# Moving twelve tiles of a mixture-of-experts matmul out of a recurrent loop and behind it

## What is computed

```python
def cell(h, x):
    gi = x @ W_ih + b_ih
    gh = h @ W_hh + b_hh
    i_r, i_z, i_n = jnp.split(gi, 3, axis=-1)
    h_r, h_z, h_n = jnp.split(gh, 3, axis=-1)
    r = jax.nn.sigmoid(i_r + h_r)
    z = jax.nn.sigmoid(i_z + h_z)
    n = jnp.tanh(i_n + r * h_n)
    h_new = (1.0 - z) * n + z * h
    return (h_new, h_new)
...
logits = xf @ router_w + router_b
S = jax.nn.softmax(logits, axis=-1)
G, idx = jax.lax.top_k(S.T, k)          # k = 256 tokens for each expert
out = jnp.einsum('ekh,hd->ekd', tokens, expert_w) + expert_b
y = zeros.at[idx].add(G[..., None] * out)
x = x + y
```

## Time and profile before

| | us |
|---|---|
| median of 3 executions | 1153.72 (1152.94 to 1154.68) |
| the profiled execution | 1152.81 |
| its span, first to last instruction | 1150.7 |
| TensorE matmul busy | 1135.9 (99% of the span) |
| VectorE busy | 770.9 (67%) |
| ScalarE busy | 363.2 (32%) |

### The profile page before, as it was taken

One profiled execution on the slowest core, in us unless ns is written; L12 is line 12 of the kernel. 1 busy time (PEld: TensorE's weight loads), 2 busy tenths in 40 slices (PEclk: granted clock), 3 DMA queues, 4 the chain that ended last, 5 costly groups with the idle time before them and its releaser, 6 DMA issues.

```text
span 1150.7 us, 63227 instructions
## 1 busy us (share of the span) xinstructions
PE 1135.9 (99%) x28287; PEld 1002.7 (87%) x28287; DVE 770.9 (67%) x4245; ACT 363.2 (32%) x1366; POOL 6.8 (1%) x31
## 2 busy tenths in 40 slices
PE   8999999999999999999999999999999999999998
PEld 5888888888999999999999999999999999999872
DVE  3677667676666666666666666666666666666886
ACT  1333333333333232323333333333333333332440
POOL 2000000000000000000000000000000000000000
PEclk9999999999999999999999999999999999999999
DMA  6311000111111001111110011111000000000208
GB/s 242 86 22 21 13 15 20 21 22 22 21 22 22 16 10 21 21 22 22 22 22 10 17 21 22 22 22 22 16 11 11 13 12 13 4 4 3 59 17 280
DMA packets 80261, 36.93 MB, mean 32 GB/s; under 512 B 69987, under 2 KB 69987, under 8 KB 79990
## 3 DMA queue, kind: packets, MB, share of 16 engines
q1 hardware_dynamic: 77648, 28.66, 10.4%
q10 hardware_dynamic: 2342, 4.24, 1.1%
HBM read 24.49 MB, written 8.39 MB: 29 GB/s over the span
## 4 chain that ended last, share of the span: by engine, by line
PE 95%; DVE 2%; DMA 1%; issue 0%; SPq 0%; ACT 0%; DVEq 0%
PE gates L429 58%; PE gates L414 29%; PE ffn_ps L472 5%; PE gates L472 3%; DMA whh<-in_L_cond_W_hh 1%; PE log_ps L481 1%; DVE wih L717 1%; PE log_ps L554 0%; SPq L234 0%; SPq L237 0%; DVE thr_upper L738 0%; DVE reached L733 0%; PE gates L574 0%; DVE wih L764 0%; DVE u L616 0%
## 5 line engine op out<-in xcount | busy, mean ns | idle before, releaser
L429 PE MATMUL gates<-whh,tok 128*16 128x192 f32 x16384 | 716.1, 326 | 2.8 <-DMA whh<-in_L_cond_W_hh 2.4
L429 PEld LDWEIGHTS gates<-whh,tok 128*16 128x16 f32 x16384 | 601.1, 124 | 57.7 <-DMA whh<-in_L_cond_W_hh 3.2
L414 PE MATMUL gates<-wih,xT 128*32 128x192 f32 x8192 | 384.3, 327 | 0.1
L414 PEld LDWEIGHTS gates<-wih,xT 128*32 128x32 f32 x8192 | 289.7, 111 | 42.7 <-issue 0.8
L616 DVE SCALAR_TENSOR_TENSOR u<-th,gates 128x64 f32<-128x64 f32 x512 | 113.3, 221 | 302.3 <-ACT th L326 302.3
L326 ACT ACTIVATE th<-gates 128x128 f32<-128x128 f32 x512 | 140.0, 273 | 443.2 <-PE gates L429 443.2
L331 ACT ACTIVATE n_t<-v 128x64 f32<-128x64 f32 x512 | 131.2, 256 | 277.7 <-DVE v L620 277.7
L632 DVE STREAM_TRANSPOSE nT<-n_t 128x64 f32<-128x64 f32 x512 | 123.8, 242 | 0.0
L623 DVE STREAM_TRANSPOSE zT<-th 128x64 f32<-128x64 f32 x512 | 121.6, 237 | 0.0
L620 DVE SCALAR_TENSOR_TENSOR v<-u,gates 128x64 f32<-128x64 f32 x512 | 113.2, 221 | 8.8
L641 DVE SCALAR_TENSOR_TENSOR tok<-new_n,z_h 128x32 f32<-128x32 f32 x512 | 110.7, 216 | 8.7
(11 more groups left out here) (111 smaller groups left out, 147.9 us busy)
## 6 DMA issues: line engine op xcount, KB each, us to landing
x_in<-in_x SPq DMA_DIRECT2D x248, 32.0 KB, 2.1
xs<-in_x SPq DMA_DIRECT2D x26, 256.0 KB, 3.6
out<-tok SPq DMA_DIRECT2D x16, 256.0 KB, 3.8
out<-tok ACTq DMA_DIRECT2D x16, 256.0 KB, 3.9
wih<-in_L_cond_W_ih SPq DMA_DIRECT2D x4, 768.0 KB, 7.1
whh<-in_L_cond_W_hh SPq DMA_DIRECT2D x4, 768.0 KB, 12.9
whh<-in_x SPq DMA_DIRECT2D x6, 256.0 KB, 4.7
we<-in_L_ffn_expert_w SPq DMA_DIRECT2D x1, 1024.0 KB, 5.4
```

What stands on the lines that cost most here:

```text
L414: nc.tensor.matmul(gates[q % 2][a][Q * j:Q * (j + 1), IN:HN].rearrange("b (g k c) -> b g k c", g=G, k=KH), xT[:, n % 2, kc, first:first + ...
L429: mm = nc.tensor.matmul(gates[t // S % 2][a][Q * j:Q * j + rows, R_:GC].rearrange("b (g k c) -> b g k c", g=G, k=KH), columns, by_tile(whh ...
```

## The change

Four things are edited. `IN_LOOP` becomes 0, so no unit stands in the loop but for the 6 in each of the last two steps; the presets and stores of ScalarE in the loop go, and the one preset that the last steps need is issued at step 252. With `IN_LOOP = 0` the first 9 tiles are the stored ones (`IN_PSUM = 9`), and 23 tiles are read from PSUM. `PSUM_PLACES` gives these 23 their places in the order of the sums: the first five, every second one up to place 20, and the last ten. PE's wait for the layer's weights moves from step 64 to step 32.

```diff
--- before.py
+++ after.py
@@ -43,9 +43,8 @@
     PAD = P
 
 
-    IN_LOOP = 12
+    IN_LOOP = 0
     UNITS = K * 4
-    FIRST = T - IN_LOOP * UNITS
     BANKS = 5
 
     LAST_UNITS, SOFTMAX_UNITS, ROUND_UNITS, SHORT_UNITS = 6, 28, 9, 4
@@ -53,7 +52,7 @@
     EVACUATED = 9
     IN_PSUM = IN_LOOP + EVACUATED
 
-    PSUM_PLACES = [0, 1, 2, 3, 4, 9, 14, 18, 22, 27, 31]
+    PSUM_PLACES = [i for i in range(NT) if i < 5 or i % 2 == 0 or i > 21]
     stored_tiles, psum_tiles = iter(range(IN_PSUM)), iter(range(IN_PSUM, NT))
     OUT_ORDER = [next(psum_tiles if i in PSUM_PLACES else stored_tiles) for i in range(NT)]
     FFN_LOADS = (4 + NI) * 16
@@ -356,18 +355,13 @@
                 if t % S == S - 1 and t // S + 2 < NB:
 
                     set_biases(t // S + 2)
-                if t == FIRST - 2:
+                if t == T - 4:
                     act.wait_ge(ffn_w_loaded, FFN_LOADS)
                     preset_ffn(0)
-                if t > FIRST and (t - FIRST) % UNITS == 0:
-                    store_ffn((t - FIRST) // UNITS - 1)
-                if t >= FIRST and (t - FIRST) % UNITS == 2 and (t - FIRST) // UNITS + 1 <= IN_LOOP:
-                    preset_ffn((t - FIRST) // UNITS + 1)
 
 
             for n in range(IN_LOOP + 1, IN_LOOP + BANKS - 1):
                 preset_ffn(n)
-            store_ffn(IN_LOOP - 1)
             preset_ffn(IN_LOOP + BANKS - 1)
             act.wait_ge(shifted, 1)
             nc.scalar.activation(scores, scores, ACT.Exp).then_inc(soft_exp, 1)
@@ -526,10 +520,9 @@
             for t in range(T):
                 tt, q, s = t % TT, t // S, t % S
                 step(t)
-                if t == FIRST:
-                    pe.wait_ge(ffn_w_loaded, FFN_LOADS)
                 if t and t % (QUAD * TT) == 0:
                     if t == QUAD * TT:
+                        pe.wait_ge(ffn_w_loaded, FFN_LOADS)
                         pe.wait_ge(log_biased, 1)
                     router(t // (QUAD * TT) - 1)
                 if q + 1 < NB:
@@ -539,8 +532,6 @@
                         project(q + 1, s, kc)
                 else:
                     expert(LAST_UNITS)
-                if t >= FIRST:
-                    expert(1)
             expert(2)
             pe.wait_ge(h_ready[1], T)
             router(NT // QUAD - 1)
```

## The result

The changed kernel takes 1151.95 us in the median (20 executions, 1150.65 to 1154.12), the kernel before 1153.67 us (20 executions, 1152.17 to 1156.29). The ratio is 0.9985, with a 95% interval of 0.9979 to 0.9992: 0.15% faster, less than the 0.2% that was set as the bound of "the same". The prediction was 1152.1 us, with 0.82 on "the same". The profiled execution took 1151.28 us, with a span of 1149.1.

A forecast was written before the change was run, and what follows sets the result against it. TensorE was taken as the bound: -41.9 us in the loop and +41.2 in the tail give -0.7, the last transfer -0.9, together -1.6 us from 1153.72: 1152.1 us, range 1150.8 to 1153.8.

The forecast's parts named there:

- Steps: In the loop: removing 192 units at 0.218 us each saves 41.9 us, with steps of 3.90 us.
- the margin of 0.06 us for the state: At a loop step's start: state written before the weight load needing it; margin falls from 0.24 to 0.06 us, stays positive.
- Tail: Behind the token weights: 12 added tiles of wide groups at 3.434 us each cost 41.2 us; TensorE net -0.7 us.
- Transfers: Output transfers at the end: more time for the same bytes, last lands sooner; -0.9 us, bounds 0 to -1.0.
- Rival 1: At the end: the last transfer gains nothing, only -0.7 us remains, 1153.0 us; chance 0.13.
- Rival 2: Tail or loop: wide tiles cheaper than read, or loop saves more; sum -2.3 us, 1151.4 us; chance 0.13.
- Rival 3: At a loop step's start: state chain becomes the bound; at 30 ns a step +4.2 us, 1157.9 us; chance 0.04.
- Rival 4: In the 68 us behind the token weights: TensorE's clock falls, 3.43 us more per tile, two give 1159.0; chance 0.03.

The follow-up runs named there:

- the kernel with useless work in the wait: The changed kernel plus 20 matmuls of 128 columns into a spare PSUM bank, in TensorE's wait ahead of the token weights: 1151.10 us, ratio 0.9981.
- quiet-end: The kernel before with ten of its 32 output transfers left out, at places 19 to 30 of the order: 1153.44 us, ratio 0.9997.
- crowded-end: The changed kernel with six 256 KB loads issued by SyncE behind its last output transfer and waited for at the end: 1155.94 us, ratio 1.0021.
- the other order of the sums: The changed kernel summing four PSUM tiles, then all nine stored tiles, then the other 19 PSUM tiles: 1152.18 us, ratio 0.9985.

## Why the prediction was right

**Steps.** The price of a unit in the loop was 0.218 us as read, and with the margin of 0.06 us for the state no step of the stretches read was longer than 3.900. One unit of the 192 was not on the path: the one of the last step, which stands ahead of the last router, and that waits for the last state anyway. The timeline shows the router with `[0.27 <-DVE tok L632]` after the change and with no wait of TensorE before it. So 191 units, 41.7 instead of 41.9 us, were saved; that is 0.2 us of the sum.

**Tail.** 12 tiles for 41.20 us, predicted 41.2. TensorE's end moved by 0.53 us, predicted 0.7. The rest of the difference is small change: the start of the loop came 0.14 us later (step 64 ends at 275.68 instead of 275.54) and the search ran 0.19 us shorter (49.54 instead of 49.73). The start is luck: the kernel with useless work in the wait, whose clock did not fall in the first steps, ends step 64 at 274.81, 0.87 us earlier than the changed kernel's profile. Over all 14 profiles step 64 ends between 274.81 and 276.62.

**Transfers.** Predicted -0.9 within -1.0 to 0; measured -1.1, just outside these bounds. The bound was read from transfers that landed in 2.9, and I took less than the whole of it; the last one lands in 2.8. The quiet-end and crowded-end kernels show the mechanism from both sides. Rival 1 fell.

**Rival 2** (the kernel gains 2.3 us because wide tiles are cheaper than read) fell: 3.433 us a tile with empty queues and with full ones. The rule of the Trainium skill ("TensorE: Matmul & The Clock Gate", section "Wait — 56ns, not 53.3ns?"), a fixed cost of about 2.5 ns for each matmul, does not suffice here: the price of a narrow unit depends on what stands around it (0.218 alone, 0.234 in a row), which a fixed cost for each matmul does not describe.

**Rival 3** fell with the steps of 3.900. **Rival 4** (the clock falls in the tail) was wrong in its place and its weight. I put it at pauses between banks, which don't exist. The clock does fall in the tail, in a part of the executions, but at the start of it, behind the wait for the chosen tokens, and with the list of the kernel before as well as with the changed one. The prediction read the clock from one profile in which it had stayed up, and did not ask whether the idle time of 1.27 us ahead of the weights left it so in every execution. It did not hurt, since both kernels have the wait.

The number came out so close by two small errors of opposite sign, 0.2 us too much on TensorE and 0.2 too little at the last transfer, and by luck: the interval of the ratio allows any gain from 0.9 to 2.4 us, and a fall of the clock moves a single execution by as much as the whole gain.

## What to carry to other kernels

When one engine is the bound from start to end, moving its work from one place to another is worth only the difference of the two prices; read both from rows where the instruction has the neighbours it will have, since the same unit cost 0.218 us between wider products and 0.234 in a row. Look for gains where that engine waits: five units put into 1.3 us of its idle time gained 1.4 us, nearly as much as the twelve tiles moved (1.7), and 21 units put into its waits, as wide groups, gained 3.9. And read what is behind an idle stretch in more than one execution, because a fall of TensorE's clock may be in only some of them.

## What the runs showed of the hardware

- TensorE's clock fell to 1.2 GHz behind an idle time of 1.27 us ahead of eight short products, in five of nine profiles (in one of the other four the idle time was 1.32 us), and cost 1.6 to 1.7 us where wide groups followed; with 0.18 to 0.25 us idle in its place it did not in five profiles. Filling the wait with work that nobody reads lowered the median by 0.85 us.
- It also fell at 20 to 24 us, behind waits for the loads of `W_hh`, in 5 of 14 profiles, whatever the kernel.
- A unit of four 128-column products costs 0.218 us alone between 192-column products and 0.231 to 0.234 in a row; a quarter of a group of four 512-column products costs 0.215.
- An output transfer of 256 KB lands in 2.8 us when it is the last of a quiet end (DMA share 0.27 to 0.34), in 3.9 at a DMA share of 1.00 by stores of its own kind, and in 5.3 among six loads of the same size.
- In the changed kernel's profile TensorE stood for 1.1 us in the middle of its narrow units at 1030.96, for nothing that the profile shows (`[1.09 <-issue]`), beside the six late loads of `x`. It fell into time in which TensorE waited anyway. A stop of 0.91 us stands near the same place in the profile with the other order of the sums. Its cause was not tried.
